# Another order for a batch of attention work: 3,2,3,2,3,2,2,2,3,2 units to the chunks, seven value runs, keys and turns in other chunks

## The reference

```python
x = x + xattn(layernorm(x), ctx, ctx, mask, W_q, W_k, W_v, W_o)
x = x + ffn(layernorm(x), gate_w, w1, w2)

def xattn(Q, K, V, mask, W_q, W_k, W_v, W_o):
    q, k, v = heads(Q @ W_q.T), heads(K @ W_k.T), heads(V @ W_v.T)
    scores = einsum('bhqd,bhkd->bhqk', q, k) / sqrt(8)
    e = exp(clip(scores, -50, 50)); e = where(mask, e, 0)
    return merge(einsum('bhqk,bhkd->bhqd', e / sum(e), v)) @ W_o.T

def ffn(x, gate_w, w1, w2):
    p = softmax(x @ gate_w); top2 = the two largest, scaled to sum 1
    return sum over the two of weight * (gelu(x @ w1[e]) @ w2[e])
```

## Time and profile before

| | |
|---|---|
| median of three runs | 1077.06 us (1076.58 to 1077.75) |
| the profiled execution: its own time | 1075.98 us |
| its span on the core | 1074.1 us |
| TensorE matmul busy | 1009.1 us, 94% |
| TensorE weight load busy | 755.5 us, 70% |
| VectorE busy | 772.0 us, 72% |
| ScalarE busy | 769.7 us, 72% |
| granted TensorE clock, mean | 0.971 |

### The profile page before, as it was taken

The page is one execution under the profiler, slowest core; times in us unless marked ns, Lnnn a source line. Parts: engine busy times, 40 slices in busy tenths (PEclk is TensorE's granted clock), DMA queues, the critical chain, the costliest instruction groups (busy, mean ns, idle before and its releaser), DMA issues.

```text
span 1074.1 us, 32328 instructions
## 1 busy us (share of the span) xinstructions
PE 1009.1 (94%) x10544; PEld 755.5 (70%) x10545; DVE 772.0 (72%) x2100; ACT 769.7 (72%) x1088; POOL 222.2 (21%) x310
## 2 busy tenths in 40 slices
PE   4899999999999999999999999999999999499980
PEld 3677777777777777777777777777777765399980
DVE  4877777777777777777777777788777876344433
ACT  2788888888888888888888888888888886144430
POOL 3301111111111111111111111111111112155554
PEclk8899999999999999999999999999999999699995
DMA  7545555555555555555555555555555554122216
GB/s 216 181 159 173 174 169 171 171 179 179 179 179 179 179 179 179 179 179 179 179 175 172 177 171 174 171 176 175 176 177 177 178 163 147 29 70 63 64 46 183
DMA packets 156606, 172.71 MB, mean 161 GB/s; under 512 B 48618, under 2 KB 100846, under 8 KB 156574
## 3 DMA queue, kind: packets, MB, share of 16 engines
q1 hardware_dynamic: 150526, 165.26, 47.5%
q0 software_dynamic: 4896, 6.63, 2.0%
q10 hardware_dynamic: 1152, 0.41, 0.2%
HBM read 36.83 MB, written 22.08 MB: 55 GB/s over the span
## 4 chain that ended last, share of the span: by engine, by line
PE 91%; DMA 2%; SPq 2%; ACT 1%; issue 1%; DVE 1%; POOL 0%; ACTq 0%; POOLq 0%; DVEq 0%
PE scores L735 31%; PE o_sum L747 27%; PE scratch L672 8%; PE scratch L661 7%; PE scores L855 5%; PE scores L866 5%; PE scratch L657 4%; PE scratch L708 1%; SPq L535 1%; ACT probs L972 1%; PE scratch L713 1%; DMA q_rep<-q_parts 1%; PE scratch L666 1%; PE scratch L729 1%; DMA xT_and_ctx<-expert_outputs 1%
## 5 line engine op out<-in xcount | busy, mean ns | idle before, releaser
L972 ACT ACTIVATE probs<-scores 128x800 f32<-128x800 f32 (+1 forms) x640 | 604.9, 973 | 110.6 <-PE scores L735 104.2
L1118 DVE TENSOR_SCALAR probs<-probs 128x800 f32<-128x800 f32 (+1 forms) x640 | 410.9, 663 | 63.0 <-ACT probs L972 55.8
L735 PE MATMUL scores<-q_stack,k_stack 128*128 128x400 f32 x1536 | 427.9, 385 | 8.6 <-DMA q_stack<-q_rep 5.7
L735 PEld LDWEIGHTS scores<-q_stack,k_stack 128*128 128x128 f32 x1536 | 248.3, 190 | 111.4 <-issue 52.8
L747 PE MATMUL o_sum<-probs,v_both 128*17 128x200 f32 x6144 | 309.6, 334 | 0.0
L747 PEld LDWEIGHTS o_sum<-probs,v_both 128*17 128x17 f32 x6144 | 154.7, 97 | 123.3 <-issue 47.5
L617 POOL DMA_INDIRECT expert_rows<-rows,row_atu x64 | 75.2, 1175 | 464.2 <-DVE row_atu L1215 235.9
L672 PE MATMUL scratch<-w_turned,ctxT 128*128 128x128 f32 x768 | 102.0, 276 | 0.0
L672 PEld LDWEIGHTS scratch<-w_turned,ctxT 128*128 128x128 f32 x768 | 100.3, 192 | 0.2 <-DVE v_both L1055 0.2
L661 PE MATMUL scratch<-ctxT,w_turned 128*128 128x512 f32 x186 | 85.2, 567 | 0.0
L1055 DVE COPY v_both<-scratch 128x512 f32<-128x512 f32 x93 | 63.8, 686 | 10.8 <-PE scratch L672 10.8
(11 more groups left out here) (146 smaller groups left out, 750.5 us busy)
## 6 DMA issues: line engine op xcount, KB each, us to landing
k_stack<-k_hi SPq DMA_DIRECT2D x192, 256.0 KB, 2.7
k_stack<-k_lo SPq DMA_DIRECT2D x192, 256.0 KB, 2.7
expert_rows<-fill SPq DMA_DIRECT2D x32, 406.2 KB
xT_and_ctx<-in_ctx_dram SPq DMA_DIRECT2D x16, 704.0 KB
ctx_nat<-in_ctx_dram SPq DMA_DIRECT2D x16, 704.0 KB
q_rep<-q_parts SPq DMA_DIRECT2D x124, 50.0 KB, 1.9
q_stack<-q_rep SPq DMA_DIRECT2D x124, 50.0 KB
v_both<-expert_rows SPq DMA_DIRECT2D x57, 65.0 KB, 1.8
```

What stands on the lines that cost most here:

```text
L735: last = nc.tensor.matmul(score_banks(c)[:, m, :], k_stack[p][:, g, t * P:(t + 1) * P], q_stack[p][:, g, :, :], start=True, stop=True)
L972: nc.scalar.activation(probs_of(c), score_banks(c), ACT.Exp, scale=SCALE).then_inc(exp_ready, 1)
L1118: nc.vector.tensor_scalar(chunk, chunk, LOW, HIGH, ALU.max, ALU.min).then_inc(probs_ready, 1)
```

## The change

Four tables of constants are replaced; no instruction is written differently, and each batch issues the same ones. The chunks of three units are now 0, 2, 4 and 8 of each ten (before 2, 4, 6 and 8). The 24 halves form seven runs, of 3, 4, 5, 3, 2, 1 and 6 halves, in chunks 7, 10, 13, 15, 18 and in chunks 0 and 2 of the next batch; before they formed eight, of 2, 1, 3, 4, 3, 3, 6 and 2, in chunks 7, 8, 11, 14, 16, 18 and in chunks 1 and 3 of the next. The turns go from chunks 0, 0, 10 to 0, 2, 9, the keys from 10, 11, 11 to 1, 12, 12, the values from 4, 6, 12 to 3, 5, 17, `heads` from 5 to 4, `tokens` from 14 to 13; `query` stays in 9 and stands behind a turn there; `queries`, `project`, `gate` and `rank` stay in 7, 8, 15 and 19.

```diff
-    UNITS = [2, 2, 3, 2, 3, 2, 3, 2, 3, 2] * 2
+    UNITS = [3, 2, 3, 2, 3, 2, 2, 2, 3, 2] * 2
-    HALF_AT = [7, 7, 8, 11, 11, 11, 14, 14, 14, 14, 16, 16, 16, 18, 18, 18, 21, 21, 21, 21, 21, 21, 23, 23]
+    HALF_AT = [7, 7, 7, 10, 10, 10, 10, 13, 13, 13, 13, 13, 15, 15, 15, 18, 18, 20, 22, 22, 22, 22, 22, 22]
-    STEPS = [("turn", 0), ("turn", 1), ("value", 0), ("heads", 0), ("value", 1), ("queries", 0),
-             ("project", 0), ("query", 0), ("turn", 2), ("key", 0), ("key", 1), ("key", 2),
-             ("value", 2), ("tokens", 0), ("gate", 0), ("rank", 0)]
-    STEP_AT = [0, 0, 4, 5, 6, 7, 8, 9, 10, 10, 11, 11, 12, 14, 15, 19]
+    STEPS = [("turn", 0), ("key", 0), ("turn", 1), ("value", 0), ("heads", 0), ("value", 1),
+             ("queries", 0), ("project", 0), ("turn", 2), ("query", 0), ("key", 1), ("key", 2),
+             ("tokens", 0), ("gate", 0), ("value", 2), ("rank", 0)]
+    STEP_AT = [0, 1, 2, 3, 4, 5, 7, 8, 9, 9, 12, 12, 13, 15, 17, 19]
```

## The result

The changed kernel takes 1065.17 us, the median of four runs (1063.66 to 1066.95), against 1077.2 for four runs of the kernel before (1076.58 to 1077.75): a ratio of 0.9891, 95% interval 0.9876 to 0.9906. It is faster by 12.0 us, 10.1 to 13.4 by the interval. The forecast was 7.8 us, 1069.3, and the range ended at 1067.0: the sign was right and the gain too small. The profiled execution is the slowest of the four: 1066.95 us, span 1065.1.

A forecast was written before the change was run, and what follows sets the result against it. The prediction took TensorE's pieces, without waits, to bound the kernel. Saving 0.32 - 0.02 - 0.02 = 0.28 us over 29 batches gave -8.1, first two 0, last +0.3: -7.8, median 1069.3 us, range 1067 to 1073.8.

The forecast's parts named there:

- What bounds the kernel: Middle batches: a batch costs what its pieces cost on TensorE in this order, without waits, 27.52 us.
- TensorE is not the bound: Rival for the whole kernel: the saved switch turns into idle time and the time stays at 1077; chance 0.06.
- The price of a run: Value runs on TensorE: each costs 0.32 us besides its halves, so eight becoming seven saves 0.32 a batch.
- lateness: Scores 8 in chunk 7 and scores 13 in chunk 12 wait for exponentials, 0.02 us each a batch.
- The rows show one such cost.: TensorE's pieces in a batch: of costs that depend on neighbours, only the 0.13 + 0.19 us for each run was seen.
- The walk: Chunk-by-chunk reckoning of a batch: scores against exponentials, steps against copies; it gave 27.52 us for the order before.
- The last batch: Final batch, six steps only, paced by ScalarE: 0.3 us longer, between -0.3 and +1.
- The first two: First two batches: saved runs set against one more unit in the first chunk and waits; 0, between -0.6 and +1.
- the rival by which these copies cost 0.40: Chunk 9: turn's and query's copies served late before scores 13, a batch 0.10 us longer, 1080; chance 0.07.
- the dearer places: Rival: scores 8 and 13 each cost 0.1 us more, or a third place joins: 1072 to 1075; chance 0.15.
- The rival without lateness: Rival: scores 8 and 13 are not late, 29 x 0.32 = 9.3 us saved, near 1068; chance 0.12.
- The signs of being wrong: Middle batch: period over 27.4, scores 13 over 0.1 us late, other waits, or a run's 0.32 moving to the next piece.

The follow-up runs named there:

- experiment 1: The kernel before with the gate step alone moved from chunk 15, between scores, to chunk 16, ahead of a value run: 1072.68 us, ratio 0.9964.
- experiment 2: The changed kernel with the gate step alone moved from chunk 15 back between scores, to chunk 16: 1068.05 us, ratio 0.9917.
- experiments 3 and 5: First: kernel before, chunk 8's single half joined to chunk 7's run, 1079.06 us. Second: changed kernel, rank step moved to chunk 18 ahead of a run, 1064.87 us.
- experiment 7: A new order with six value runs, gate and rank both ahead of a run, units as in the kernel before: 1053.0 us, ratio 0.9776.
- experiment 8: A new order with five value runs, units as in the changed kernel, query in chunk 1: 1056.37 us, ratio 0.9802.
- experiments 9 and 10: The changed kernel with the gate's product 128 columns wide instead of 8: first ahead of the run, 1067.16 us; then between scores in chunk 16, 1069.25 us.

## Why the prediction was wrong in size

**What bounds the kernel** held. Where an experiment's period changed, the chain or the timeline shows the pieces of TensorE or the waits that changed it. The rival "TensorE is not the bound" falls with experiment 1: a step of TensorE moved, 0.100 us a batch gone. The rule of the Trainium skill that stood with it, "Perfetto Trace Analysis", "Identifying the Most-Contended Engine", isn't borne out here, as far as it goes by weight loads: by them (70% beside 72%) TensorE was not the engine to look at, and the period followed its pieces. The other measure that the Trainium skill gives there, the share of peak arithmetic (MFU), was not worked out.

**The price of a run** held. With the gate between scores in both orders (the kernel before and experiment 2) the period falls by 27.514 - 27.199 = 0.315, which is the 0.32 forecast less the small lateness.

**The step that failed is "The rows show one such cost."** There was a second one. Turns, keys and values were costed at nothing for their place, the query at one price "wherever it stands", and the gate, which the change also moves to other neighbours, was not priced by place at all. Its price stood in the chain of before, 0.10 and then 0.47 for two units, and no term of the prediction takes it up. It is worth 0.100 a batch in the order before (experiment 1) and 0.107 in the new one (experiment 2), 2.9 to 3.1 of the 4.1 us by which the middle batches saved more than forecast.

**The lateness** was over-priced: scores 8 about 0.01 and scores 13 none, against 0.02 and 0.02. The walk had put the first late by 0.02 and the second even within the digits of its rows, so the mechanism was no surprise, only the side; 29 x 0.03 = 0.9 us. The figure of the Trainium skill, "ScalarE: Activation LUTs", "What ACT_TABLE_LOAD costs", would have made both places later, and its 1071 is farther off than the sum from the rows. What then remains of the 4.1 us, 0.1 to 0.3, is at most 0.01 a batch, the rounding of the pieces.

**The rest.** The last batch came out at +0.30 as forecast; that is one profile, no run tested the walk behind it, and so close a match is partly luck. The first two lost 0.43 where 0 was taken, inside its bounds. ScalarE's order in chunk 9 went as walked. Its timeline after:

```profile
319.06 0.51 ACT L910 COPY ctxT<-scratch 128x420 f32<-128x420 f32 x1 [0.36 <-PE scratch L657]
319.47 0.25 ACT L921 COPY q_full<-scratch 128x100 f32<-128x100 f32 x1
319.60 1.92 ACT L972 ACTIVATE probs<-scores 128x1200 f32<-128x1200 f32 x2
```

The turn's copy, the query's and the two exponentials end 2.46 us behind the first start, and 0.39 + 0.17 + 1.90 was the sum: the rival by which these copies cost 0.40 did not come. Nor did the dearer places. The rival without lateness was nearly right on lateness and would still have missed by 3 us, for want of the gate.

The range failed for the same reason. Its lower end was built from the run's price and the ends of the kernel alone, so a gain that no term named could not lie in it. The signs of being wrong had the same gap: each looked for a smaller gain, and none of them came. The upper end, 1073.8, is 0.3 above the middle of 1072 to 1075 that it was taken from; the result doesn't test it.

## What to carry to other kernels

When an order is changed on an engine that never waits, price every piece by what stands behind it, also the shortest: read each kind of piece in all the neighbourhoods that the trace has, and note which ones differ. A short piece that seems free can be cover for another engine's work: two single moves that saved time on TensorE (experiments 3 and 5) gave it back as a wait for an exponential. So walk the whole order with the measured prices; one built that way (experiment 7) gained twice what the change gained, and another (experiment 8) fell 0.25 us a batch short of its forecast where its sum had no waits for ScalarE.

## What the runs showed of the hardware

A pair of 8-column products costs TensorE 0.20 us between scores (the kernel before and experiment 2) and 0.10 directly ahead of a run of 17-column weights (experiment 1); ahead of a value projection the 0.10 shows as 0.99 for 0.89 (experiment 8). At 128 columns the pair costs 0.22 in both places (experiments 9 and 10), so that a product 16 times as wide is dearer by only 0.02 between scores.

A run of 17-column products among full-width ones costs 0.32 us besides its products, at the full clock: with the gate between scores in both orders, one run less took 0.315 us off the period, with other pieces moved as well (the kernel before and experiment 2).
